# A fused attention and feed-forward kernel: reciprocal roots moved to GpSimd, all instruction lists in a new order

## The reference

```
x = x + attention(layernorm(x), ctx, ctx, lengths)
x = x + ffn(layernorm(x))

attention:  8 heads; for each head the 256 columns of x and of ctx are the
            sequence, 16 of the 128 rows are the head's dimension
            s = SCALE * log(length of the batch)
            out = softmax(s * q^T k) v
ffn:        2 experts, each 256 -> 1024 -> 256
            h = x W_fc;  a = (h if h >= 0 else 0.5 h)^2;  y = a W_proj
            the router picks one expert per row and weighs its output
layernorm:  (x - mean) / sqrt(var + 1e-5) over the 256 columns
```

## Time and profile before

| | us |
|---|---|
| median of three runs | 173.63 |
| lowest and highest run | 172.86 and 173.75 |
| span of the profiled execution (the page gives no other time of it) | 170.4 |
| TensorE busy in the span | 161.4 (95%) |
| DVE busy | 129.2 (76%) |
| ACT busy | 97.0 (57%) |
| POOL busy | 58.6 (34%) |

### The profile page before, as it was taken

One profiled execution on the slowest core, in us unless ns is written; L12 is line 12 of the kernel. 1 busy time (PEld: TensorE's weight loads), 2 busy tenths in 40 slices (PEclk: granted clock), 3 DMA queues, 4 the chain that ended last, 5 costly groups with the idle time before them and its releaser, 6 DMA issues.

```text
span 170.4 us, 4075 instructions
## 1 busy us (share of the span) xinstructions
PE 161.4 (95%) x1494; PEld 139.9 (82%) x1494; DVE 129.2 (76%) x301; ACT 97.0 (57%) x181; POOL 58.6 (34%) x68
## 2 busy tenths in 40 slices
PE   7998887899999989999989999999999999999992
PEld 7986745487698869896978798969879999999991
DVE  7799987999898999995999867953179875056442
ACT  4444979558659956957346526943794065335220
POOL 7331544630322420372521260405023253136330
PEclk9999999999999999999999999999999999999999
DMA  4577857794468054004501460002010000010001
GB/s 120 167 241 246 259 190 233 217 292 126 143 229 251 3 161 120 14 19 139 174 0 62 125 189 4 0 0 67 0 62 0 4 0 0 4 61 0 0 4 62
DMA packets 18883, 16.98 MB, mean 100 GB/s; under 512 B 1776, under 2 KB 18672, under 8 KB 18864
## 3 DMA queue, kind: packets, MB, share of 16 engines
q1 hardware_dynamic: 18144, 16.00, 30.3%
q10 hardware_dynamic: 720, 0.73, 1.5%
HBM read 8.72 MB, written 1.05 MB: 57 GB/s over the span
## 4 chain that ended last, share of the span: by engine, by line
PE 75%; DVE 11%; issue 4%; SPq 3%; ACT 3%; DMA 2%; DVEq 0%; ACTq 0%
PE hp L1358 25%; PE ops L1388 22%; PE pv L1342 6%; PE stp L1318 6%; PE ops L1273 5%; DVE negm L813 5%; PE snp L1265 3%; DMA x_raw<-x 2%; ACT probs L514 2%; DVE a_lo L921 2%; PE ops L1376 2%; PE pv L1376 1%; PE stp L1324 1%; PE pv L1398 1%; PE snp L1301 1%
## 5 line engine op out<-in xcount | busy, mean ns | idle before, releaser
L378 POOL TENSOR_TENSOR a_buf<-l_buf 128x512 f32<-128x512 f32 x32 | 35.7, 1119 | 77.8 <-DVE a_lo L921 44.6
L514 ACT ACTIVATE probs<-stp,scale_b 128x1024 f32<-128x1024 f32 x30 | 33.4, 1114 | 14.8 <-PE stp L1318 11.3
L1358 PE MATMUL hp<-xt_hi,wfc_hi 128*128 128x256 f32 x128 | 37.2, 291 | 0.0
L813 DVE TENSOR_REDUCE negm<-snp 128x4 f32<-128x1024 f32 x28 | 34.1, 1218 | 3.6 <-PE snp L1265 3.4
L1358 PE MATMUL hp<-xt_hi,wfc_lo 128*128 128x256 f32 x128 | 35.8, 279 | 0.0
L1358 PE MATMUL hp<-xt_lo,wfc_hi 128*128 128x256 f32 x128 | 35.7, 279 | 0.0
L522 ACT ACTIVATE l_buf<-hp 128x512 f32<-128x512 f32 x32 | 18.8, 594 | 23.7 <-PE hp L1358 17.0
L921 DVE TENSOR_TENSOR a_lo<-a_buf,a_hi 128x512 fp32r<-128x512 f32 x32 | 26.2, 831 | 7.6 <-ACT a_hi L529 6.2
L1358 PEld LDWEIGHTS hp<-xt_hi,wfc_hi 128*128 128x128 f32 x128 | 24.0, 188 | 2.1 <-issue 1.0
L1388 PE MATMUL ops<-wproj_hi,a_hi 128*128 128x256 f32 x112 | 23.6, 292 | 0.5 <-DVE wproj_lo L953 0.5
L1358 PEld LDWEIGHTS hp<-xt_hi,wfc_lo 128*128 128x128 f32 x128 | 24.1, 188 | 0.0
(11 more groups left out here) (112 smaller groups left out, 237.2 us busy)
## 6 DMA issues: line engine op xcount, KB each, us to landing
k_st<-k_hi SPq DMA_DIRECT2D x16, 128.0 KB, 2.1
wfc_raw<-w_fc_t SPq DMA_DIRECT2D x8, 256.0 KB, 4.4
wproj_raw<-w_proj_t SPq DMA_DIRECT2D x8, 256.0 KB, 3.5
q_st<-q_hi SPq DMA_DIRECT2D x14, 128.0 KB, 2.1
x_raw<-x SPq DMA_DIRECT2D x8, 128.0 KB, 3.0
k_st<-k_lo SPq DMA_DIRECT2D x8, 128.0 KB, 2.4
v_raw<-ctx_t SPq DMA_DIRECT2D x8, 128.0 KB, 2.6
x_keep<-x SPq DMA_DIRECT2D x8, 128.0 KB, 2.7
```

The lines of the kernel that those rows point to most:

```text
L378: pool.tensor_tensor(a_buf[d % 2][:, :, :], l_buf[d % 2][:, :, :], l_buf[d % 2][:, :, :], ALU.mult).then_inc(s_a, 1)
L514: act.activation(probs[g][:, :, :, :], pair[:, :, :].rearrange("p e (c n) -> p e c n", c=KC), ACT.Exp, scale=scale_b[:, b:b + 1]).then_inc ...
L813: dve.tensor_reduce(negm[b % 2][:, :, :, g].rearrange("p c e -> p e c"), pair[:, :, :].rearrange("p e (c n) -> p e c n", c=KC), AX.X, ALU. ...
L1358: last = pe.matmul(hp[:, d % 2, half], wfc[w][:, kc, c * P:(c + 1) * P], xt[:, kc, :], start=(c % 2 == 0 and kc == 0 and w == 0 and xt is ...
```

## The change

Three things change together.

**The reciprocal root.** ACT's `x_ln`, `x_rstd`, `y_ln` and `y_rstd` and DVE's `newton` go, with their tiles and semaphores. In their place POOL computes (var + eps) to the power -0.5 in one instruction on 128x1 elements, `x_scale` or `y_scale`; the exponent is a tile `expo` that DVE fills once. The third stage of the moments now only adds eps, and waits for the power of two batches earlier before it writes again.

```
+            def x_scale(b):
+                j = b % 2
+                if b == 0:
+                    pool.wait_ge(s_expo, 1)
+                pool.wait_ge(s_xvar, b + 1)
+                wait(pool, s_qf, b - 1)
+                pool.tensor_tensor(xsc[j][:, :], xvar[j][:, :], expo[:, :], ALU.pow).then_inc(s_xsc, 1)
+            def y_scale(b):
+                j = b % 2
+                pool.wait_ge(s_yvar, b + 1)
+                wait(pool, s_x2n, b - 1)
+                pool.tensor_tensor(ysc[j][:, :], yvar[j][:, :], expo[:, :], ALU.pow).then_inc(s_ysc, 1)
...
-            def x_ln(b):
-                act.wait_ge(s_xvar, b + 1)
-                act.activation(xln[b % 2][:, :], xvar[b % 2][:, :], ACT.Ln, scale=-2.0).then_inc(s_xln, 1)
-            def x_rstd(b):
-                act.wait_ge(s_xln, b + 1)
-                act.activation(xrs[b % 2][:, :], xln[b % 2][:, :], ACT.Exp, scale=-0.5).then_inc(s_xrs, 1)
...
+            def fill_expo():
+                dve.memset(expo[:, :], -0.5).then_inc(s_expo, 1)
...
-                    dve.tensor_scalar(var[:, :], mv[:, 1:2], EPS, -0.5, ALU.add, ALU.mult).then_inc(s_var_, 1)
-            def newton(stage, b, var, rs, n1, sc, s_rs_, s_n1_, s_sc_):
-                if stage == 0:
-                    dve.wait_ge(s_rs_, b + 1)
-                    dve.scalar_tensor_tensor(n1[:, :], rs[:, :], rs[:, 0:1], var[:, :], ALU.mult, ALU.mult).then_inc(s_n1_, 1)
-                else:
-                    dve.wait_ge(s_n1_, b + 1)
-                    dve.scalar_tensor_tensor(sc[:, :], n1[:, :], 1.5, rs[:, :], ALU.add, ALU.mult).then_inc(s_sc_, 1)
+                    wait(dve, s_used, b - 1)
+                    dve.tensor_scalar(var[:, :], mv[:, 1:2], EPS, None, ALU.add).then_inc(s_var_, 1)
```

**The order of all five lists.** Apart from the steps above, the same calls stand in each list, in another order. On ACT's list the start now reads:

```
+            load_consts()
             load_kv(act, 0)
-            load_consts()
             load_kv(act, 1)
+            pick_rows()
             k_part_hi(0)
-            x_ln(0)
-            x_rstd(0)
             q_part_hi(0)
...
-            pick_rows()
```

More of the change, by code:

```diff
@@ L427, in _ @@
             square(1, 5)
+            y_scale(4)
+            y_scale(5)
             square(1, 6)
+            place_v(6)
+            place_v(7)
             square(1, 7)
             square(2, 0)
-            place_v(7)
             square(2, 1)
@@ L436, in _ @@
             square(2, 5)
+            y_scale(6)
+            y_scale(7)
             square(2, 6)
@@ L612, in _ @@
-            exp(2, 2)
-            k_part_hi(4)
+            leaky(0, 0)
+            split_w(1, 1)
+            square_hi(0, 0)
             exp(2, 3)
-            leaky(0, 0)
-            square_hi(0, 0)
-            q_part_hi(5)
+            split_w(1, 2)
+            max_rows(3)
+            split_w(1, 3)
             leaky(0, 1)
-            split_w(1, 1)
-            max_rows(3)
+            exp(3, 0)
+            leaky(0, 2)
+            k_part_hi(5)
             square_hi(0, 1)
-            split_w(1, 2)
@@ L623, in _ @@
-            leaky(0, 2)
-            exp(3, 0)
+            exp(3, 1)
             square_hi(0, 2)
-            x_ln(7)
-            x_rstd(7)
-            exp(3, 1)
+            exp(3, 2)
             leaky(0, 3)
+            exp(3, 3)
+            square_hi(0, 3)
+            k_part_hi(6)
+            k_part_hi(7)
             coef_exp(0)
-            split_w(1, 3)
-            square_hi(0, 3)
-            exp(3, 2)
-            k_part_hi(5)
-            leaky(0, 4)
-            exp(3, 3)
-            max_rows(4)
@@ L638, in _ @@
[L638 to L640 removed]
+            split_w(1, 4)
+            split_w(1, 5)
+            split_w(1, 6)
+            split_w(1, 7)
+            max_rows(4)
+            leaky(0, 4)
             leaky(0, 5)
[L642 removed]
             square_hi(0, 4)
[L644 to L645 removed]
+            exp(4, 0)
             square_hi(0, 5)
[L647 removed]
+            q_part_hi(6)
+            exp(4, 1)
+            exp(4, 2)
@@ L1046, in _ @@
             row_max(3, 0)
-            x2_newton(1, 0)
-            x2_newton(1, 1)
             x2_normalise(1)
+            q_part_lo(4)
             row_max(3, 1)
-            x_newton(5, 0)
             xt_part_lo(0)
-            x_newton(5, 1)
-            router_diff()
-            q_normalise(5)
             row_max(3, 2)
-            q_part_lo(4)
+            x_moments(6, 0)
+            x_moments(6, 1)
+            row_max(3, 3)
+            split_max_hi(3)
+            split_max_lo(3)
```

761 lines of the change are left out of this document (347 added, 414 removed).

## The result

The changed kernel takes **171.26 us** (median of 20 runs, 170.10 to 173.48) against 172.73 for before (20 runs); the ratio is **0.9907, 95% interval 0.9888 to 0.9926**: faster by 0.9%. I forecast 172.9, within 171.3 to 175.2: the time came out lower, just outside the range. The gain that I forecast was 0.73 us; 1.47 were measured. (Ratios leave out executions in which the chip ran disturbed, medians do not, so the two can differ by some tenths of a per cent.)

The account below looks back on a forecast made before the run. DVE was taken to bound the kernel up to x_transpose(0) at 39.8 us, TensorE's matmuls behind it. From 173.63 us, -0.9 ahead, +0.2 for a shape turn and 0.0 for idle gave 172.9, range 171.3 to 175.2.

Parts of the forecast that it names:

- the base: Starting time of the whole-kernel sum: the median of before's runs, taken as 173.63 us.
- Nearly all of it is matmuls that no order can shorten.: From x_transpose(0) to the last output step, TensorE's 127.1 us were taken as almost wholly fixed work.
- two ways of gaining: A reordering could gain only by an earlier x2_normalise(1) or from TensorE's 1.23 us of idle between 39.8 and 89.
- Idle of the same size as before, 1.2 to 1.5 us: Behind x_transpose(0), TensorE would wait as much in the new order as in the old; a 0.0 term.
- +0.2 for one more switch: Behind x_transpose(0), one more turn between score shapes and full ones slows first matmuls by 0.1 us each side.
- `x_transpose(0)` 0.9 earlier: At the border to feed-forward work, less DVE work from 27.9 us on brings the start near 38.9; -0.9 us.
- The start was as worked out: At the program start, later k_hi puts q_f at 6.3, first scores at 9.1, batch 0's last nm_r 0.7 later.
- so `row_max(2, 0)` starts at 27.9, as in before: From 14 to 27.9 us, the shorter DVE list is eaten by the later start, leaving this reduction's start unchanged.
- come about when they did: Batch 2's first stack issue (21.69) and the scores it releases (27.35) were expected at about before's times.
- 3.2 us lie around the span: Difference between the 173.63 us median and the profiled 170.4 us span, assumed unchanged.
- The power: Each new GpSimd power was put at 0.3 us, between 0.103 and 1.275, mostly hidden behind other work.
- slower through the power: Rival: powers of 1.275 us delay the start and the second normalisation of a pair, giving 175.3 us; some 2 in 10.

Follow-up runs that it names:

- new_old_addresses: The changed kernel plus two unused tiles, so every larger tile lies where it lies in before; no instruction or order changed; ratio 0.9985.
- two_items: The kernel before with two entries of TensorE's list moved, max_transpose(4) one feed-forward chunk later and ffn1(1, 7) ahead of ffn2(0, 14); ratio 1.0016.
- the first round: First group of follow-up kernels, asking whether the new order or the GpSimd powers made the gain; ratios to before from 0.9928 to 1.0374.
- new_again: The changed kernel unaltered, measured and profiled a second time beside runs of before; ratio 0.9941.
- newton_new_order: The changed kernel with the old inverse-root path back (ScalarE logarithm and exponential, DVE Newton steps, no GpSimd powers), otherwise the new order; 179.67 us, ratio 1.0374.
- stacks_first: The changed kernel with keep(0) and load_weights(0, 3) moved behind the six stack transfers of batch 1 in SyncE's list; ratio 1.0069.
- stacks_first_2: stacks_first with ScalarE's split_w(0, 3) also moved behind exp(0, 2); 170.80 us, ratio 0.9877.

## Why the prediction was wrong, point by point

The direction was right, the places were not. The forecast was -0.9 ahead of `x_transpose(0)`, +0.2 and 0.0 behind it; the two profiles show +0.18 ahead and -1.49 behind. Two terms failed with opposite signs, and the base was too high; that the sum came out within 1% is luck.

- **"Nearly all of it is matmuls that no order can shorten."** This is the step that put the gain in the wrong place, and with it fell the limit to two ways of gaining. Those matmuls ran 1% faster. There are 768 feed-forward matmuls (128 chunks of six); 768 x 1.2 ns is 0.92 us, and new_old_addresses shows 1.04. It isn't the order's doing: on balance the change took 11 small tiles out of the allocation. The diff showed that; I didn't ask what it moves.
- **"Idle of the same size as before, 1.2 to 1.5 us."** Wrong: with the 1.04 taken off, 0.45 of the 1.49 us are left. The waits shown behind 40 us fell from 1.23 to 0.61, and to none from 62 us on. two_items shows that moving entries by itself would not do this.
- **+0.2 for one more switch.** Not settled: the waits fell by 0.62 and the stretch, pace apart, by 0.45. The 0.17 between is of the size of this term, but no run separates it.
- **`x_transpose(0)` 0.9 earlier.** Wrong: 40.01, 40.98 and, with early stacks, 39.58. The start was as worked out: q_f 6.06 (6.3), first scores 9.02 (9.1), last `nm_r` 14.50 (14.5). The last part was right too: from `row_max(2, 0)` to `x_transpose(0)` it was 39.83 - 27.89 = 11.94 us before and is 40.01 - 28.93 = 11.08 now, 0.86 less. What failed lies between, "so `row_max(2, 0)` starts at 27.9, as in before": it came at 28.93, 1.04 later, and ate the 0.86. I had the last `nm_r` of batch 0 come 0.7 later and still let the stacks of batch 2 "come about when they did". But the exponentials that free their buffer start behind that `nm_r`: the first came at 16.52 and not 15.80, and the first stack of batch 2 was issued at 22.76 and not 21.69. So some 0.7 of the 1.04 was in my own sum. The rest is added on the way: `scores_qk(1, 0)`, whose stacks I put near 16.6, ran at 17.76, and `scores_kq(0, 1)`, the next link of the chain of exponentials, stood behind it. ScalarE's timeline of before:

```profile
15.80 1.11 ACT L514 ACTIVATE probs<-stp,scale_b 128x1024 f32<-128x1024 f32 x1 [0.57 <-PE stp L1324]
```

- **The base.** The sum starts from 173.63, the median of three runs; over 20 runs before takes 172.73. That makes 0.90 of the 1.64 us by which the forecast missed, and the other 0.74 is the gain. That "3.2 us lie around the span" was a sign of it: in the 21 runs of before beside the first round each run is 1.75 to 2.32 us longer than its own span, so a span of 170.4 belongs to some 172.4 us. I had set the span of one execution beside the time of others.
- **The power.** 0.55 and 0.58 us on the mean, not 0.3, within the bounds. It shows as one wait of DVE, 0.45 at 17.15, and DVE waits another 0.41 for scores ahead of `row_max(1, 0)` at 18.31, so no cost is seen. The rival "slower through the power" needed 0.7. The first power took 0.56. (The Trainium skill, GPSIMD Engine Reference, section 2.1 "Instruction dispatch", gives some 6 us for the first call of a freshly loaded function; this trace shows no such time.)

What the powers and the order are worth apart from addresses isn't settled. With before's addresses the whole change is 0.9985 (0.9951 to 1.0019), no difference that can be told; before with the new addresses is 0.9975; powers on top of that 0.9928; the order on top of these 0.9907 or 0.9941. The intervals of neighbours in this row overlap, and the runs stem from different sessions, each held against its own runs of before. What is shown is that the last stretches and the 1.04 us behind the border follow the addresses.

## What to carry to other kernels

Compare the pace of the same matmuls in a stretch without waits before naming a wait: a busy TensorE can still be 1 to 3% slower. When a change adds or removes a tile, even of four bytes, look at what it does to the addresses behind it, and pad to tell the two apart. Take a time and a span from the same execution, and a base from more than three runs. When a chain starts later, carry the delay through to its end. And when a transfer is moved, follow every instruction that stands behind the one that waits for it, on every engine.

## What was not expected of the hardware

- Matmuls of 128x256 elements with fp32r operands took 116.7 to 117.2, 118.0 to 118.3 or 120.3 ns each by where their operands lie relative to each other within 128 bytes of a partition: fastest at 64, slowest at 0. Moving both together changed nothing (24.47 us). Only feed-forward tiles were moved apart from their weights; the cause inside the chip isn't shown.
- A wait of TensorE of 1.74 us ahead of 18.73 (new_again) left the granted clock at 1.00, and so did one of 2.12 us ahead of 32.27 (newton_new_order). One of 1.81 us ahead of 18.72 (new_old_addresses) was followed by 0.56 from 20 to 22 us, and one of 2.27 us ahead of 19.73 (stacks_first) by 0.50, 1.2 GHz. The length of the wait alone doesn't tell which. stacks_first_2 starts the scores of batch 1 at 16.46 without a wait.
- A GpSimd power of 128x1 takes 0.55 us, five times a memset of that size (0.103).
